# A gated cross-attention layer with routed feed-forward: later weights, loads in the order of need, and another order at the feed-forward's start

## The reference

```python
q = split_heads(layernorm(x) @ Wq + bq)        # 16 heads of 16
k = split_heads(ctx @ Wk + bk); v = split_heads(ctx @ Wv + bv)
scores = where(mask, -1e15, q @ k.T / sqrt(16))
x = x + tanh(g_xattn) * (softmax(scores) @ v @ Wo + bo)
y = layernorm(x)
h = tanh(mean(y, rows) @ W1 + b1); probs = softmax(h @ W2 + b2)     # 8 zones
top 3 zones of each item, weights w renormalised
x = x + tanh(g_ffn) * (y + sum_e w_e * gelu(y @ Wa[e]) @ Wb[e])     # Wa 256x1024, Wb 1024x256
```

## Time and profile before

| | us |
|---|---|
| median of 3 runs (lowest, highest) | 348.01 (347.06, 348.06) |
| the profiled execution | 344.57 |
| its span, first to last instruction | 342.5 |
| PE, DVE, ACT, POOL busy | 294.1, 202.3, 195.2, 159.4 |
| mean granted TensorE clock | 0.975 |

### The profile page before, as it was taken

One profiled execution on the slowest core, in us unless ns is written; L12 is line 12 of the kernel. 1 busy time (PEld: TensorE's weight loads), 2 busy tenths in 40 slices (PEclk: granted clock), 3 DMA queues, 4 the chain that ended last, 5 costly groups with the idle time before them and its releaser, 6 DMA issues.

```text
span 342.5 us, 9360 instructions
## 1 busy us (share of the span) xinstructions
PE 294.1 (86%) x3348; PEld 243.5 (71%) x3348; DVE 202.3 (59%) x617; ACT 195.2 (57%) x406; POOL 159.4 (47%) x217
## 2 busy tenths in 40 slices
PE   1819679799999989989979855798899999999996
PEld 1415457577676766767756535798899999999996
DVE  7226857476687776867676331655555664456452
ACT  3223666777767767777776863453466345445432
POOL 3725896859978699786989872001000000000000
PEclk9967999999999999999999996999999999999999
DMA  6953877857767687674764340100100101001000
GB/s 160 299 145 109 225 203 176 220 166 194 220 161 231 174 220 211 168 223 120 219 154 142 82 138 0 42 3 22 48 23 21 42 3 43 26 20 42 2 15 15
DMA packets 33180, 40.53 MB, mean 118 GB/s; under 512 B 10248, under 2 KB 26944, under 8 KB 33136
## 3 DMA queue, kind: packets, MB, share of 16 engines
q1 hardware_dynamic: 26416, 22.16, 24.6%
q0 software_dynamic: 4784, 16.98, 16.6%
q10 hardware_dynamic: 1936, 0.79, 0.9%
HBM read 33.09 MB, written 6.74 MB: 116 GB/s over the span
## 4 chain that ended last, share of the span: by engine, by line
PE 56%; DMA 13%; POOL 10%; ACT 7%; issue 6%; DVE 3%; SPq 2%; DVEq 1%; ACTq 0%; POOLq 0%
PE bank L1219 16%; PE bank L1238 16%; PE bank L1064 7%; DMA k_scr<-wb 4%; DMA qbd<-q_scr 4%; POOL wb L460 3%; DMA stage<-in_L_ffn_Wb 3%; PE bank L1014 3%; POOL wa L460 3%; POOL stage L455 2%; PE bank L1026 2%; PE bank L1073 2%; PE bank L1046 2%; PE bank L1030 2%; ACT pT L545 2%
## 5 line engine op out<-in xcount | busy, mean ns | idle before, releaser
L769 DVE CUSTOM_DVE_ANT_0 bank<-bank,maskb 112x375 f32<-112x375 f32 x128 | 67.9, 571 | 44.2 <-PE bank L1014 44.1
L1219 PE MATMUL bank<-ctxT,wqkvo 128*128 128x112 f16 x960 | 61.4, 216 | 10.9 <-DVE qbd L944 10.9
L1219 PEld LDWEIGHTS bank<-ctxT,wqkvo 128*128 128x128 f16 x960 | 59.0, 100 | 12.5 <-issue 12.1
L1238 PE MATMUL bank<-wb,stage 128*112 x576 | 66.8, 273 | 0.0
L1238 PEld LDWEIGHTS bank<-wb,stage 128*112 128x112 f16 x576 | 62.3, 130 | 0.2
L732 ACT ACTIVATE kst<-bank 128x448 f32<-128x448 f32 x48 | 25.7, 535 | 57.1 <-PE bank L1219 57.0
L545 ACT ACTIVATE pT<-bank 125x448 f32<-125x448 f32 x96 | 48.7, 539 | 7.1 <-PE bank L1030 6.4
L943 DVE COPY wqkvo<-wa 128x3072 f16 x24 | 23.2, 966 | 42.7 <-PE bank L1219 38.2
L1014 PE MATMUL bank<-kst,qbd 128*112 128x375 f16 x128 | 33.2, 334 | 16.5 <-DMA qbd<-q_scr 13.3
L455 POOL TENSOR_SCALAR stage<-stage 128x512 f32<-128x512 f32 x64 | 39.6, 631 | 13.1 <-DMA stage<-in_L_ffn_Wb 6.4
L460 POOL TENSOR_TENSOR wa<-stage,wa 128x512 f16<-128x512 f32 x32 | 37.0, 1167 | 12.9 <-ACT wa L655 12.3
(11 more groups left out here) (125 smaller groups left out, 449.6 us busy)
## 6 DMA issues: line engine op xcount, KB each, us to landing
stage<-in_L_ffn_Wa POOLq DMA_DIRECT2D x16, 512.0 KB, 4.4
stage<-in_L_ffn_Wb POOLq DMA_DIRECT2D x16, 512.0 KB, 5.2
kst<-k_scr SPq DMA_DIRECT2D x64, 93.8 KB, 3.6
k_scr<-wb SPq DMA_DIRECT2D x16, 187.5 KB
ctx_s<-in_ctx SPq DMA_DIRECT2D x8, 336.0 KB
qbd<-q_scr SPq DMA_DIRECT2D x32, 56.0 KB, 3.7
xa<-in_x SPq DMA_DIRECT2D x8, 112.0 KB, 4.3
q_scr<-wb SPq DMA_DIRECT2D x16, 56.0 KB, 3.2
```

The source lines that it names most:

```text
L769: v.tensor_tensor_reduce(out=bank[0:SQ, e, 0:SK], in0=bank[0:SQ, e, 0:SK], in1=maskb[0:SQ, b % 2, 0:SK], scale=-1.0, scalar=FLOOR, op0=ALU ...
L1219: ins = T.matmul(o, first(ws, t, f), x2b[:, b % 2, (xs * DT + t) * SQ:(xs * DT + t + 1) * SQ], start=(t == 0 and xs == 0 and ws == 0), sto ...
L1238: ins = T.matmul(o, hT[:, u % 2, hs * FT * SQ + f * SQ:hs * FT * SQ + (f + 1) * SQ], wb[:, bass.ds(e * (4 * CHUNK) + ws * (2 * CHUNK) + f ...
```

## The change

- `parts_at`: no parts in slots 0 and 1 of b = -1, then 2 in every slot; the last are in slot 1 of b = 7.
- SP: ctx before x; the biases bk and bq there; the mask before the next ctx; Wv, Wo, bv and the gates only after `read_q(0, 0)` of the first iteration, before `read_k(0, 1)`. ACT issues only Wk and Wq. `tanh_gates` moves to slot 1 of b = -1.
- POOL: the first three part loads and the constants only when half 0 of item 0's K and Q has been read back.
- DVE: `vp` and `pT` are filled after `q_lo(0)`, `maskb` after the first context copy.
- TensorE: `busy(n)` issues n products of `ident` with itself into a bank that nobody reads; 9 before the loop, 24 after slot 1 of b = -2.
- Border: `copy_weights(0)` before `residual(6)`; `normed2(6)` behind `hidden(0)`; another spread of the rest over the zones.

```diff
-            n = min(2 if i < 0 or j < 3 else 1, NPART - at)
+            n = min(2 if (i, j) >= (-1, 2) else 0, NPART - at)
-TAIL = (("X2T", B - 2), ("OT", B - 1), ("ON", B - 1), ("OP", B - 1), ("X2T", B - 1), ("H", 1), ("L", 1), ("W", 1))
+TAIL = {0: ("OT", B - 1), 1: ("X2T", B - 2), 2: ("ON", B - 1), 3: ("OP", B - 1), 5: ("X2T", B - 1), 7: ("H", 1), 8: ("L", 1), 11: ("W", 1)}
...
+            load_ctx(0)
             load_x(0)
-            load_ctx(0)
-            sp.dma_start(wqkvo[:, 2, :, :], view_w(Wv)).then_inc(s["wv_loaded"], 16)
+            sp.dma_start(bk_c...)
+            for t in range(DT):
+                sp.dma_start(bq_c...)
...
                 load_xr(o)
+                load_mask(m)
                 load_ctx(m + 1)
                 load_x(m + 1)
-                load_mask(m)
...
                 read_k(m, 0)
                 read_q(m, 0)
+                if b == -2:
+                    sp.dma_start(Wv), sp.dma_start(Wo), sp.dma_start(bv_c), sp.dma_start(gates) twice
...
             norm1(0)
-            for k in range(0, RING, 2):
-                load_parts(k)
...
                 for slot in range(4):
+                    if (b, slot) == (-1, 0):
+                        pool.wait_ge(kq_in[0][0], 96)
+                        for k in range(0, RING, 2):
+                            load_parts(k)
+                        g.dma_start(bo_r), (w1_s), (w2_s), (b1_c), (b2_r)
...
-                if u == 0:
+                if u == 1:
                     x2_hi(B - 2)
                 if u == 2:
                     ot_copy(B - 1)
-                if u == 3:
+                if u == 4:
                     normed2(B - 1)
-                if u == 4:
+                if u == 5:
                     x2_hi(B - 1)
-                if u == 5:
+                if u == 7:
                     route_hidden(1)
-                if u == 6:
+                if u == 9:
                     route_exp(1)
...
+                if b == B - 1:
+                    dve.wait_ge(s["idx_loaded"], 16)
+                    dve.wait_ge(s["hi_done"], NPART)
+                    dve.wait_ge(s["lo_done"], NPART)
+                    full(dve, ("V1", B - 1))
+                    dve.wait_ge(s["pe_st"], tile(B - 1, 0, 0))
+                    copy_weights(0)
                 residual(o)
...
                 low(u)
                 if u == 0:
+                    o_rows(B - 1)
                     result(B - 2)
+                if u == 2:
                     x2_lo(B - 2)
-                if u == 1:
-                    o_rows(B - 1)
-                if u == 3:
+                if u == 4:
                     residual(B - 1)
-                if u == 4:
+                if u == 5:
                     result(B - 1)
+                if u == 6:
                     x2_lo(B - 1)
-                if u == 6:
+                if u == 9:
                     route_logits(1)
-                if u == 7:
+                if u == 10:
                     route_top(1)
-                if u == 8:
+                if u == 12:
                     route_shares(1)
...
+            def busy(n):
+
+                for i in range(n):
+                    T.matmul(bank[:, ST_BANKS[i % 2], 0:128], ident[:, :], ident[:, :], start=True, stop=True)
...
             pe.wait_ge(s["ident_ready"], 1)
-            pe.wait_ge(s["zeroed"], 3)
+            busy(9)
...
+                    if (b, slot) == (-2, 1):
+                        busy(24)
...
             g1(0)
+            put(TAIL[0])
...
-                if u < 7:
+                if u > 0 and u in TAIL:
                     put(TAIL[u])
-                if u == 8:
-                    put(TAIL[7])
                 g2(u, e)
```

More of the change, by code:

```diff
@@ L97, in __init__ @@
                     names.append(name)
-        for i, name in enumerate(TAIL):
+        for i, name in enumerate(TAIL.values()):
             names.append(name)
@@ L409, in _ @@
                 read_q(m, 0)
+                if b == -2:
+                    sp.dma_start(wqkvo[:, 2, :, :], view_w(Wv)).then_inc(s["wv_loaded"], 16)
+                    sp.dma_start(wqkvo[:, 3, :, :], view_w(Wo)).then_inc(s["wo_loaded"], 16)
+                    sp.dma_start(bv_c[:, :], bv.rearrange("(t p) -> p t", p=128), allow_slow_non_contiguous=True).then_inc(s["bv_loaded"], 16)
+                    sp.dma_start(gates[:, 0:1], bass.AP(g_xattn.tensor, 0, [[0, 128], [1, 1]])).then_inc(s["g_loaded"], 16)
+                    sp.dma_start(gates[:, 1:2], bass.AP(g_ffn.tensor, 0, [[0, 128], [1, 1]])).then_inc(s["g_loaded"], 16)
                 store_r(b - 2)
@@ L495, in _ @@
                             base=-CK, pattern=[[0, 1]], channel_multiplier=1).then_inc(s["ones_ready"], 1)
[L496 to L504, removed]
             for b in range(-2, B):
                 for slot in range(4):
+                    if (b, slot) == (-1, 0):
+                        pool.wait_ge(kq_in[0][0], 96)
+                        for k in range(0, RING, 2):
+                            load_parts(k)
+                        g.dma_start(bo_r[:, :], bass.AP(bo.tensor, 0, [[0, 128], [1, D]])).then_inc(s["const_loaded"], 16)
+                        g.dma_start(w1_s[:, :, :], W1.rearrange("(t p) n -> p t n", p=128)).then_inc(s["const_loaded"], 16)
+                        g.dma_start(w2_s[:, :], W2).then_inc(s["const_loaded"], 16)
+                        g.dma_start(b1_c[:, :], b1.rearrange("(p o) -> p o", o=1), allow_slow_non_contiguous=True).then_inc(s["const_loaded"], 16)
+                        g.dma_start(b2_r[:, :], bass.AP(b2.tensor, 0, [[0, B], [1, NZ]])).then_inc(s["const_loaded"], 16)
                     ks = parts_at(b, slot)
@@ L515, in _ @@
                         norm1(b + 3)
+                    if (b, slot) == (-2, 3):
+                        pool.wait_ge(s["zeroed"], 4)
+                        sums = vp[:, :, KC - 1, :, HD]
+                        g.affine_select(out=sums, in_=sums, compare_op=ALU.not_equal, fill=SK * TINY,
+                                        base=-CK, pattern=[[0, 2], [0, NH]], channel_multiplier=1).then_inc(s["ones_ready"], 1)
                     for k in ks:
@@ L526, in _ @@
             a = nc.scalar
+            a.dma_start(wqkvo[:, 1, :, :], view_w(Wk)).then_inc(s["wk_loaded"], 16)
             a.dma_start(wq_in, view_w(Wq)).then_inc(s["wq_loaded"], 16)
[L528 to L535, removed]
             def exp_tile(b, g, c):
@@ L697, in _ @@
                     w_hi(k)
+                if b == -1:
+                    tanh_gates()
                 if b == B - 1:
@@ L886, in route_shares, with copy_weights @@
                 v.tensor_copy(wbc[:, b0 * TOPK:(b0 + n) * TOPK], spare_bank(("W", g))[:, 0:n * TOPK]).then_inc(s["wbc_done"], 1)
+            def copy_weights(u):
+                if u == ROUTES[1][0] * TOPK:
+                    dve.wait_ge(s["idx_loaded"], 32)
+                e = dve.value_load(idx_row[0:1, u:u + 1], min_val=0, max_val=NZ - 1)
+                need(dve, s["g1_done"], 2 * u)
+                v.tensor_copy(wst3, wa[:, bass.ds(e * (4 * CHUNK), 3 * CHUNK)]).then_inc(s["wst_done"], 1)
+                v.tensor_copy(wst1, wa[:, bass.ds(e * (4 * CHUNK) + 3 * CHUNK, CHUNK)]).then_inc(s["wst_done"], 1)
             v.memset(qbd[:].rearrange("p a e j f -> p (a e j f)"), 0.0).then_inc(s["zeroed"], 1)
-            v.memset(vp[:].rearrange("p a c h i -> p (a c h i)"), 1.0).then_inc(s["zeroed"], 1)
+            ln1_stats(0)
             v.memset(bank[:, O_BANK, :], 0.0).then_inc(s["zeroed"], 1)
[L891 to L894, removed]
             for b in range(-2, B):
@@ L898, in _ @@
                 cx_copy(m)
+                if b == -2:
+                    v.memset(maskb[96:KQ, :, :], 1.0).then_inc(s["zeroed"], 1)
                 row_max(n, 1)
@@ L912, in _ @@
                 q_lo(m)
+                if b == -2:
+                    v.memset(vp[:].rearrange("p a c h i -> p (a c h i)"), 1.0).then_inc(s["zeroed"], 1)
+                    v.memset(pT[96:CK + 1, :, :], 1.0).then_inc(s["zeroed"], 1)
+                    dve.wait_ge(s["zeroed"], 5)
                 result(b - 2)
@@ L1038, in pv @@
                     pe.wait_ge(s["act_exp"], tile(b, g, 2) + 1)
+                    if b == 0 and g == 0:
+                        pe.wait_ge(s["zeroed"], 2)
                     if g == 0:
```

21 lines of the change are left out of this document (4 added, 17 removed).

## The result

| | before | after |
|---|---|---|
| median of 20 runs each, us | 347.95 | 347.95 |
| lowest and highest, us | 342.39, 353.17 | 344.56, 352.38 |
| profiled execution, us | 344.57 | 345.69 |
| span of it, us | 342.5 | 343.6 |

The ratio after : before is 1.0091, with the interval 1.0053 to 1.0129. It leaves out the executions that lie more than 1.5% above the fastest of their kernel, 2 of the 20 after and 11 of the 20 before, while the medians of all 20 agree. No measurement shows it faster; whether it is slower stays open. Predicted were 335.3 us, 3.7% faster.

The account below looks back on a forecast made before the run. The prediction saw no single limit: a chain of waits bounds the start, POOL the attention loop, POOL's end and DVE's copies the border. Gains 7.45 + 3.45 + 1.8 = 12.7 took 344.57 to 331.9, plus 3.4 gave 335.3 us; range 329.5 to 343.

Parts of the forecast that it names:

- K at 10.1: Start: with x landing at 5.8 behind ctx, the first K product starts at 10.1 us, 0.1 later than before.
- Clock in K and Q, 1.35: Start: K and Q may run at 2.4 GHz; half of K's 2.65 us saving taken, 1.35 us (bounds 0 and 3.2).
- busy(24), 1.6: Start: unread products after Q keep batch 1's projections, transposes and scores at 2.4 GHz, 1.6 us gained (0.5 to 2).
- Fills later 0.3: Start: later 512 KB loads leave batch 0's K write and read alone, 0.3 us gained (0 to 1).
- batch 1's transfers 0.9: Start: batch 1's write and read run with two fills fewer beside them, 0.9 us gained (-1 to 2.5).
- Cover about 1 us, behind it 3 us of slack ... All that is nil.: Start: Wv, Wo, bv and gates ahead of read_k(0, 1) on SP add 2.4 us of issue but cost nothing.
- POOL's schedule +2.8: Attention loop: 7 more parts and 3 load issues, 15.2 us of work less 12.6 of waits, 2.8 us longer with batch 0.
- Border 7.45: Attention to feed-forward: copy_weights(0) before residual lets g1(0) start at 201.85 in place of 209.31, 7.45 us earlier.
- 3.45 to g1(2): After the border: g1(2) comes 9.05 us after g1(0) starts in place of 12.5, 3.45 us gained (bounds 2 and 4).
- Tail 1.8: Feed-forward: stalls of 1.03 and 1.01 us go, less 0.2 us for the second index store, 1.8 us gained.
- B: Rival, start: x lands late and the clock stays low; start gain 0.8 in place of 4.05 us, 338.6 us; chance 0.20.
- C: Rival, loop: POOL becomes the bound with its waits kept, 2.90 us a part, 350.7 us, slower; chance 0.08.

Follow-up runs that it names:

- y2: x4 with more unread TensorE products (8 after ctx's transposes, 3 after x's, 36 in place of 24 behind Q): 339.18 us, ratio 0.9775.
- b3: b2 with unread TensorE products added (9 at the start, 2 after ctx's transposes, 3 after x's, 36 after Q): 336.82 us, ratio 0.9719.
- y1: x4 without the 9 and 24 unread TensorE products: 341.08 us, ratio 0.9876.
- b2: z2 with x1's index store move and one more weight part in each of items 0 to 2, taken from item 7: 337.97 us, ratio 0.9718.
- x2: Changed kernel, with POOL's fills and constants waiting for half 1 of item 0's K and Q, not half 0: 344.84 us, ratio 0.9976.
- x3: Changed kernel, with Wv, Wo, bv and both gates issued behind the reads of half 1 on SP: 344.04 us, ratio 0.9888.
- x4: Changed kernel, with only the tiny loads (bv and two gates) back on ACT's queue at the start: 339.98 us, ratio 0.9756.
- c1: Changed kernel, with Wv, Wo, bv and gates loaded at the start and the second index store moved later: 338.45 us, ratio 0.9749.
- z1: Kernel before, with the new weight part schedule (`parts_at`) alone: 350.05 us against 347.32, ratio 1.0039.
- z2: Kernel before, with the new order of border and tail alone: 342.17 us, ratio 0.9838.
- x1: Changed kernel, with the store of the second index one iteration later on SP's queue: 347.56 us against 347.29, ratio 0.9989.

## Why the prediction was wrong

The sum had 12.7 us of gain; 1.1 us of loss came, a miss of 13.8 us between profiled spans: 12.05 of it in the start, 1.9 in the loop, 0.3 in the border's gap, and 0.45 the other way in the rest. By its own steps:

1. **K at 10.1**: 10.65. x was costed to land at 5.8, its statistics began at 6.51, and normed and CX0 followed in the time given. Mechanism right, 0.5 us late.
2. **Clock in K and Q, 1.35; busy(24), 1.6**: K's products took 5.35 us, the lower bound of the gain, and item 1's projections ran at 1.2 GHz again: nothing in place of 2.95. The Trainium skill's page weighed there (TensorE: Matmul & The Clock Gate, Part 4: PE-mode transpose) leads to the same outcome, but so does the 0.97 us of work in 3.5; no run separates them. What the prediction didn't see is that K's clock gives little: y2 and b3 have it, and item 0's scores start at 24.3 and 25.1, against 25.0 and 24.4 without added products (y1, b2). At item 1's scores 1.0 (y2) and 2.2 us (b3) are seen, but no ratio shows a gain: b3's interval is b2's, and y2's overlaps y1's. The write of K landed between 20.6 and 21.5 in all of these, however early it was issued.
3. **Fills later 0.3, batch 1's transfers 0.9**: K's write took 3.97 against 4.19, 0.2. Batch 1's scores came at 50.0 instead of 44.9, for the reason of step 4.
4. **"Cover about 1 us, behind it 3 us of slack ... All that is nil."** This is the step that failed. The added issue time was near right (2.6 us against 2.4). The landing was taken as 7 to 8 us after the first scores; it was 15.4 us after them (40.4 less 25.0). The pieces, 512 and not 384, had no price beyond their issue, and the same change starts three 512 KB fills at 25.25, as half 0 lands, just when the pieces are under way. x2 takes the fills away from there and x3 the group of loads, and s1(0, 4) is at 33.4 and 33.1, so it needs both; x4 takes the tiny pieces away alone and gets 5.1 of the 7 us. Start in all: -8.0 in place of +4.05, 12 of the 13.8 us. Of the remaining 1.6 us at s1(0, 4), x4 waits 1.2 for half 1; with Wv and Wo loaded early too, c1 has no such wait and starts 0.7 earlier, by one profile, and its time is x4's within the interval.
5. **POOL's schedule +2.8**: +4.7, the term that was mis-sized beside step 4. The period of 21.5 us, the waits for fills under 4 us (0.5) and the aligned pairs are as predicted. What came on top is at the end: from item 7's LN1 step to norm2's, 42.9 became 45.1 (z1: 45.7), 2.3 us that the sum by parts had spread over waits. z1 shows the same growth without the new start.
6. **Border 7.45**: of it 1.25 were to come from start and loop and 6.2 from the gap; the gap gave 5.9. It needs both halves: the order alone leaves 6.2 of the gap (z2), the part schedule alone 3.95 (z1), the two together 0.4. **3.45 to g1(2)**: 3.4. **Tail 1.8**: 2.3, the two stalls gone and 0.22 of new wait against 0.2 predicted. POOL ended before TensorE. Right in mechanism and size.

Of the rivals, B (the start gives nothing) named the late x and the low clock, both seen, but ended at 338.6 because it took the loads ahead of half 1 as free as well. C's mechanism, waits kept in POOL, did not occur: its waits for fills went away, and five periods of 107.6 us for 40 parts are 2.69 us a part, against 2.65 forecast and C's 2.90. What came out, not faster, had 0.12 in all and stood there for another reason.

The parts one by one, against the kernel before: border and tail -1.6%, part schedule alone +0.4% (unclear), border with a gentler schedule -2.8%, all of the change with the tiny pieces early -2.4%, all of it +0.9% by its ratio and none by the medians (x1: -0.1%).

## What to carry to other kernels

Cost a moved DMA by its number of pieces and by what else is released at that moment on other queues, not by its bytes: 2 KB in 512 pieces, beside three 512 KB fills, cost 5.6 us at the first landmark here. Where a stage ends in a write and a read of DRAM, look in a trace whether an earlier write also lands earlier before paying for a faster product. A good part and a bad part of a change can cancel to nothing, so split the span at landmarks first.

## What the runs showed of the hardware

- SP's queue moved 325 pieces under 512 bytes in the microsecond before the fills' packets came and 147 in the three after it, at 2.3% of the engines' time, while POOL's 82 packets of 4 KB took 48.1%. The loads of bv and the gates landed 5.7, 5.3 and 7.9 us after their issue, and 3.5, 3.3 and 4.1 us in x2, without the fills. The Trainium skill (DMA: Bandwidth & Descriptors, Queues, rings and completion order) has descriptors taken in ring order on each engine, which agrees with half 1's reads landing behind the tiny pieces (40.4 us, and 35.3 without them).
- Issuing slows down too: SP needed 4.51 us for four issues behind the tiny pieces with the fills beside them, 1.83 with the pieces alone (x2) and 1.85 with the fills alone (x4).
- The granted clock in b3: TensorE was busy for 15.06 of 20.5 us, the clock was at 2.4 GHz all that time, and it was lost at 26.2, as at 26.7 in the kernel after with 17 fewer added products. More fillers did not carry it to item 1's projections; why not, the runs don't say.
- One write of K to DRAM took 3.97 us (issued at 17.3, the kernel after), 4.19 (16.6, before), 5.97 (14.7, y2) and 7.39 (14.0, b3). Of these four, the earlier it was issued, the longer it took; why, the runs don't say.
